# Decoder layer with routed experts on one core: order of the work between the last cross attention and the experts

## The chip, the cores and the metric

One Trainium2 chip, one of its cores. The metric is the device time of one execution in microseconds (us), lower is better; the median of several runs is given. The engines are TensorE (PE in the profile, with PEld for its weight loads), VectorE (DVE), ScalarE (ACT), GpSimd (POOL) and SyncE (SP), which only starts transfers. Each has its own queue and runs it in order; they meet by semaphores.

## The reference

All in float32, for 16 sequences of 256 tokens and 256 features:

```python
x = x + L0_attn(layernorm(x))        # causal linear attention with exp features, 4 heads of 64,
                                     # then y -> relu(norm(y) @ W1 + b1) @ W2 + b2
x = x + L0_xattn(layernorm(x), ctx)  # q from x, k and v from ctx; softmax(q k^T / 16) v + bv
x = x + L0_ffn(layernorm(x))         # 16 experts, the best 2 of each token
# L0_ffn:
probs = softmax(xf @ Wg.T); topw, topi = top_k(probs, 2); topw = topw / topw.sum(-1)
out = sum over e of gates[:, e] * ((silu(xf @ W1[e]) * (xf @ W3[e])) @ W2[e])
```

## The kernel before, in words

A tile is 128 tokens; a sequence has TS = 2 of them, there are NSEQ = 16 sequences, numbered 0 to 15, and X holds the whole stream in SBUF. The kernel has three parts.

**Turns.** Turn i works on four sequences at once (`in_turns`, L360 and on): attention of sequence i (a), feed forward of i-1 (f), cross attention of i-2 (b), choice and places of i-3 (r). Each engine has a function `turn` with its own order of these pieces, written out by hand. Most products are made in three: a float32 value is split into hi and rest in a format for faster products (`mm3`), hi by ScalarE, rest by VectorE (`rest`). Turn 16 (`last_ffn`) has no attention; it makes the feed forward of 15, the cross attention of 14 and the places of 13. There TensorE would pause, so `keep_clock(bank, n)` (L809) issues n products of a mask with the identity, whose result nobody reads; each gives two records in the trace.

In a turn GpSimd adds the value bias bv of the cross attention to X (`add_bias`, L640), splits the next context (`split_ctx`), ranks the chosen experts (`place_rows`), and takes roots of variances for the layer norms (`root`, L633; norm 3 is the one ahead of the router). It also scatters each token's normalised row, with its number and gate, to its place in a list in DRAM that is ordered by expert (`store_rows`, L699): four indirect DMAs per sequence, two tiles by two choices, each waiting for places, gates and rows.

**Close.** `close()` on each engine has what is left: the cross attention of sequence 15, and router, choice, places and rows of 14 and 15. It works by halves (tiles), without splitting. TensorE: value product of the context, one filler, X of sequence 14 turned for its router (bank 4), the halves of xn2 turned, router of 14, queries, scores, the counts of the choice of 14 (`count_choices`), then pr turned, the weighted values, X of 15 turned, its router, three fillers, its counts. VectorE: the row constants of the scores (`row_constants`, L1722, one fused product and sum for each tile), logits and choice of 14 (`logits_in`, `choose`, `one_hot`, `row_shifts`), the scores' row maxima to snmax, gates and places of 14 (`gates`, `place_own`), then X with its statistics for 15 (L1936 to L1943), and the same choice and places for 15. ScalarE copies out of PSUM, takes the exps (`score_exp`, `gap_exp`) and writes the rows to be scattered (`whole_rows`). GpSimd's `close` (L764):

```python
store_rows(NSEQ - 3, range(1))
add_bias(NSEQ - 1, bv_sb, xn2_ready, xbv_ready, NSEQ + 1)
root(3, NSEQ - 2, eps_ln)
store_rows(NSEQ - 3, range(1, TS))
for r in (NSEQ - 2, NSEQ - 1):
    keep_rows(r)
store_rows(NSEQ - 2, range(1))
pool.wait_ge(egap_ready, NSEQ - 1)
pool.wait_ge(rows_kept, NSEQ - 2 + TS)
root(3, NSEQ - 1, eps_ln)
store_rows(NSEQ - 2, range(1, TS))
store_rows(NSEQ - 1)
```

**Plan and experts.** VectorE works out from the counts which expert each tile of 128 places belongs to (row_g, L1975; expert_i, L1984); TensorE issues nine fillers ahead of this plan's two small products and ten after it (L1240). When all scatters have landed SyncE loads the first tiles of rows, and then TensorE goes through 79 tiles: rows turned (L1197), up products, hidden turned (L1219), down products. GpSimd adds each result into the output by a scatter.

What sets the order: the hand written order of each queue, the semaphores, and PSUM banks (the router of 14 writes bank 5, the counts too).

Of the kernel before, what the change touches and what calls it, by code (L numbers as in the profile page):

```python
# [37 lines left out]
ALU = mybir.AluOpType  # L38
# [3 lines left out]
P = 128  # L42
# [5 lines left out]
def decoder(nc, x, ctxT, WqT, WkT, Wv, Wo, omegaT, W1, b1, W2, b2, gamma, beta,  # L48
# [52 lines left out]
    with ExitStack() as stack:  # L101
# [497 lines left out]
        def _(pool):  # L599
# [40 lines left out]
            def add_bias(seq, row, after, done, count=None):  # L640

                hold(pool, after, seq + 1 if count is None else count)
                xs = X[:, tiles_of(seq), :]
                pool.tensor_tensor(xs, xs, row[:, :].unsqueeze(1).broadcast_to([P, TS, D]), ALU.add).then_inc(done, 1)
# [68 lines left out]
            def turn(i, a, f, b, r, nxt):  # L713
# [28 lines left out]
                last_ffn = isinstance(i, int) and i == NSEQ  # L742
                if b is not None:
                    add_bias(b, bv_sb, xn2_ready, xbv_ready)
                    hold(pool, v2_ps, b + 1)
                    pool.wait_ge(score_ps, b + 1)
                    if last_ffn:
                        pool.wait_ge(fT_ready, NSEQ * 4)
                    split_ctx(b + 1)
# [14 lines left out]
            def close():  # L764

                store_rows(NSEQ - 3, range(1))
                add_bias(NSEQ - 1, bv_sb, xn2_ready, xbv_ready, NSEQ + 1)
                root(3, NSEQ - 2, eps_ln)
                store_rows(NSEQ - 3, range(1, TS))
                for r in (NSEQ - 2, NSEQ - 1):  # L770
# [7 lines that stand above are left out]
# [27 lines left out]
        def _(pe):  # L805
# [124 lines left out]
            def turn(i, a, f, b, r, nxt):  # L930
# [33 lines left out]
                if b is not None:  # L964
# [5 lines left out]
                    if last_ffn:  # L970
                        keep_clock(0, 8)
# [4 lines left out]
                if last_ffn:  # L976
                    keep_clock(0, 2)
# [132 lines left out]
            def close():  # L1110
# [4 lines left out]
                pe.wait_ge(x2_ready, NSEQ - 1)  # L1115
                turn_tiles(4, X[:, rows_of:rows_of + TS, :]).then_inc(xn3T_ps, 1)
# [3 lines left out]
                pe.wait_ge(counts_ready, NSEQ - 2)  # L1120
                pe.wait_ge(xn3T_ready, NSEQ - 1)
                for t in range(TS):
                    last = router_half(t, ps[:, 5, S + t * NE:S + (t + 1) * NE])
                last.then_inc(logit_ps, 1)
                for t in range(TS):
# [6 lines left out]
                    last.then_inc(q_ps, 1)  # L1132
                for t in range(TS):
# [5 lines left out]
                count_choices(NSEQ - 2)  # L1139
# [4 lines left out]
                for t in range(TS):  # L1144
# [4 lines left out]
                    last.then_inc(av_ps, 1)  # L1149
                for t in range(TS):  # L1150
                    pe.wait_ge(x2_ready, NSEQ + t)
                    turn_half(t, X[:, rows_of + TS + t, :]).then_inc(xn3T_ps, 1)
                for t in range(TS):
# [86 lines left out]
            keep_clock(2, 10)  # L1240
# [27 lines left out]
        def _(act):  # L1268
# [205 lines left out]
            def close():  # L1474
                copy_router_rows(NSEQ - 2, 4)
# [10 lines left out]
                gap_exp(NSEQ - 2)  # L1486
                act.wait_ge(zT_ps, NSEQ)
                whole_rows(rows_cross, NSEQ - 2, 0)
# [4 lines left out]
                whole_rows(rows_cross, NSEQ - 2, 1)  # L1493
# [76 lines left out]
        def _(dve):  # L1570
# [332 lines left out]
            def close():  # L1903
# [12 lines left out]
                logits_in(r, 5, S)  # L1916
                hold(dve, logit_ready, r + 1)
                choose(r)
                one_hot(r)
                row_shifts(r)  # L1920
# [6 lines left out]
                dve.wait_ge(egap_ready, r + 1)  # L1927
                gates(r)
                place_own(r)
# [14 lines left out]
                last.then_inc(mv_ready[3], 1)  # L1944
                logits_in(b, 2)
# [162 lines left out]
```

## Time and profile before

| | us |
|---|---|
| median of 3 runs | 811.09 |
| lowest, highest | 810.24, 813.86 |
| the profiled execution | 813.92 |
| its span | 812.1 |
| busy: PE, DVE, ACT, POOL | 792.2, 593.3, 435.6, 394.8 |
| mean granted clock of TensorE | 0.992 of full |

The profile is of one execution, and its rows give times from the start of the span. TensorE is busy 98% of the span, but its pauses, and the time at a lower granted clock, lie close together, around the close and the start of the experts (600 to 642 us). A row of the timeline gives start, duration, engine, line, what is written from what, how many instructions were merged, and in brackets how long the engine stood idle before it and who released it. Matmul records overlap, since they are pipelined; their distance is what they cost.

### The profile page before, as it was taken

The page shows a single profiled execution, that of the slowest core. Times are in us where ns is not written, and L with a number is a line of the kernel's source. Part 1 is how long each engine was busy: PE and PEld are TensorE (multiplying, and loading weights), DVE is VectorE, ACT ScalarE, POOL GpSimd, SP SyncE. Part 2 cuts the span into 40 slices and gives each one's busy share as a digit, 9 for nine tenths or more (in the row PEclk, how much of TensorE's full clock was granted, in tenths as well). Part 3 has the DMA queues.
Part 4 walks back from the last instruction along what each step waited for, and adds up shares of the span by engine and source line. Part 5 has one row for each costly group of instructions (what it writes and reads, how often), then busy time and mean ns, then how long its engine had stood idle before and what let it go on. Part 6 is the DMA issues. An engine that isn't in the chain of part 4 may idle for free.

```text
span 812.1 us, 20962 instructions
## 1 busy us (share of the span) xinstructions
PE 792.2 (98%) x5907; PEld 752.9 (93%) x5908; DVE 593.3 (73%) x1719; ACT 435.6 (54%) x1193; POOL 394.8 (49%) x561
## 2 busy tenths in 40 slices
PE   9999999999999999999999999999998899999995
PEld 8899999999999999999999999999896799999994
DVE  4757777888787877888887877888667466666663
ACT  4473554637274454637274554637145377667673
POOL 2432134444434354443534344443436258787876
PEclk9999999999999999999999999999999999999998
DMA  9787673755748283755748283757869357787880
GB/s 269 255 285 236 207 259 113 255 192 192 250 139 293 92 307 112 254 189 178 264 141 289 95 307 108 258 199 287 322 261 334 111 103 134 121 131 127 132 137 2
DMA packets 105961, 161.19 MB, mean 198 GB/s; under 512 B 10704, under 2 KB 69648, under 8 KB 105040
## 3 DMA queue, kind: packets, MB, share of 16 engines
q1 hardware_dynamic: 80544, 132.89, 47.8%
q0 software_dynamic: 14800, 17.61, 11.9%
q10 hardware_dynamic: 10576, 10.19, 4.7%
q8 instruction: 20, 0.33, 0.2%
q14 instruction: 21, 0.17, 0.1%
HBM read 50.14 MB, written 112.47 MB: 200 GB/s over the span
## 4 chain that ended last, share of the span: by engine, by line
PE 87%; DVE 5%; ACT 3%; issue 2%; POOL 1%; DMA 1%; POOLq 0%; DVEq 0%; SPq 0%; ACTq 0%
PE ps L807 75%; PE ps L818 5%; PE ps L1041 3%; PE ps L1197 2%; PE ps L1219 2%; ACT phi L1335 1%; ACT fT_hi L1348 1%; ACT relu_v L1349 1%; DVE pr L1724 1%; DVE xn_attn L1590 0%; DMA expert_rows<-relu_v,place_i 0%; DVE stat L1579 0%; DVE snmax L1791 0%; DVE fT_lo L1597 0%; POOL expert_rows L710 0%
## 5 line engine op out<-in xcount | busy, mean ns | idle before, releaser
L798 POOL DMA_INDIRECT out<-narrow,sidx x79 | 122.8, 1554 | 47.4 <-DVE sidx L2037 22.4
L1270 ACT ACTIVATE xn3T<-ps 128x512 f32<-128x512 f32 (+1 forms) x18 | 10.3, 574 | 141.4 <-PE ps L818 136.1
L807 PE MATMUL ps<-w_hi,fT_hi 128*128 128x256 f32 x256 | 79.9, 312 | 0.3
L1335 ACT ACTIVATE phi<-ps,nmax 128x128 f32<-128x128 f32 x256 | 73.5, 381 | 8.1 <-DVE nmax L1741 7.6
L1597 DVE TENSOR_TENSOR fT_lo<-relu_v,fT_hi 128x512 fp32r<-128x512 f32 x64 | 51.4, 802 | 31.9 <-ACT relu_v L1349 31.7
L807 PE MATMUL ps<-w_hi,fT_lo 128*128 128x256 f32 x256 | 72.4, 283 | 0.0
L807 PE MATMUL ps<-w_lo,fT_hi 128*128 128x256 f32 x256 | 72.2, 282 | 0.0
L1349 ACT ACTIVATE relu_v<-ps,b_sb 128x256 f32<-128x256 f32 x128 | 69.0, 539 | 0.0
L1348 ACT ACTIVATE fT_hi<-ps,b_sb 128x256 fp32r<-128x256 f32 x128 | 68.0, 531 | 1.0 <-PE ps L807 1.0
L807 PE MATMUL ps<-hT_hi,w_hi 128*128 128x256 f32 x256 | 67.2, 284 | 0.0
L807 PE MATMUL ps<-hT_hi,w_lo 128*128 128x256 f32 x256 | 67.0, 283 | 0.0
L636 POOL TENSOR_TENSOR veps<-mv,eps_ln 128x2 f32<-128x2 f32 x48 | 10.9, 228 | 109.4 <-DVE mv L1583 108.1
L710 POOL DMA_INDIRECT expert_rows<-rows,place_i x56 | 55.6, 992 | 15.3 <-issue 15.3
L807 PE MATMUL ps<-e_hi,xgT_hi 128*128 x158 | 58.5, 371 | 0.7 <-issue 0.6
L2031 DVE TENSOR_TENSOR hidT_lo<-ps,hidT_hi 128x256 fp32r<-128x256 f32 x79 | 33.6, 425 | 32.5 <-ACT hidT_hi L1270 31.3
L2019 DVE TENSOR_TENSOR xgT_lo<-ps,xgT_hi 128x256 fp32r<-128x256 f32 x79 | 33.5, 424 | 25.3 <-ACT xgT_hi L1270 24.4
L807 PE MATMUL ps<-hT_lo,w_hi 128*128 128x256 f32 x256 | 51.6, 284 | 0.0
L807 PE MATMUL ps<-e_lo,xgT_hi 128*128 x158 | 51.6, 328 | 0.0
L649 POOL CAST ctx_hi<-ctx_raw 128x512 fp32r<-128x512 f32 x16 | 10.4, 651 | 82.7 <-DMA ctx_raw<-in_ctxT 64.7
L807 PEld LDWEIGHTS ps<-w_hi,fT_hi 128*128 128x128 f32 x256 | 48.6, 190 | 1.9 <-DVE fT_lo L1597 1.4
L1270 ACT ACTIVATE xgT_hi<-ps 128x256 fp32r<-128x256 f32 x79 | 30.3, 384 | 36.5 <-issue 26.5
L807 PEld LDWEIGHTS ps<-hT_hi,w_hi 128*128 128x128 f32 x256 | 49.2, 192 | 0.0
(329 smaller groups left out, 2761.0 us busy)
## 6 DMA issues: line engine op xcount, KB each, us to landing
expert_rows<-zero_rows SPq DMA_DIRECT2D x16, 4352.0 KB, 16.2
narrow<-expert_rows ACTq DMA_DIRECT2D x71, 136.0 KB
expert_up_hi<-X SPq DMA_DIRECT2D x16, 352.0 KB, 2.7
e_hi<-expert_up_hi SPq DMA_DIRECT2D x2, 2816.0 KB, 10.0
part_raw<-in_E SPq DMA_DIRECT2D x30, 176.0 KB
expert_up_lo<-part_raw SPq DMA_DIRECT2D x15, 352.0 KB, 3.1
e_lo<-expert_up_lo SPq DMA_DIRECT2D x2, 2464.0 KB, 13.0
X<-in_x SPq DMA_DIRECT2D x16, 256.0 KB, 3.4
```

The lines of the kernel that those rows point to most:

```text
L710: pool.indirect_dma_start(row_dram, bass.IndirectOffsetOnAxis(place_i[:, buffer_of(r), j, t:t + 1], 0), kept[:, t, j, :], None).then_inc(p ...
L798: pool.indirect_dma_start(out_rows, bass.IndirectOffsetOnAxis(sidx[:, u:u + 1], 0), yg[:, u, :], None, bounds_check=NT * P - 1, oob_is_err ...
L807: return pe.matmul(out_, lhsT, rhs, start=start, stop=stop)
L818: last = pe.transpose(ps[:, bank, lo:lo + P], src[:, t, c * P:(c + 1) * P], ident[:, :])
L1041: last = pe.transpose(ps[:, g0 + h // 2, h % 2 * S + t * P:h % 2 * S + (t + 1) * P], phi[:, g0 + t, h, :], ident[:, :])
L1270: return act.activation(out_, in_, ACT.Copy)
L1335: last = act.activation(phi[:, g, h, :], ps[:, g, h * M:(h + 1) * M], ACT.Exp, bias=nmax[:, g, h:h + 1])
L1348: act.activation(fT[0][:, 2 * g + n, :], bank(bank_no)[:, n, :], ACT.Relu, bias=bias)
L1349: last = act.activation(relu[:, g % 2, n, :], bank(bank_no)[:, n, :], ACT.Relu, bias=bias)
L1597: dve.tensor_tensor(dst, whole, hi.bitcast(F32), ALU.subtract).then_inc(done, 1)
L2019: dve.tensor_tensor(xgT[1][:, u % 2], ps[:, u % 2, 0:D].rearrange("p (c s) -> p c s", c=DC), xgT[0][:, u % 2].bitcast(F32), ALU.subtract). ...
L2031: dve.tensor_tensor(hidT[1][:, u % 2], ps[:, 4 + u % 2, 0:2 * P].rearrange("p (c s) -> p c s", c=2), hidT[0][:, u % 2].bitcast(F32), ALU.s ...
```

## The change

It moves and edits pieces of turn 16 and of `close`:

- GpSimd: in turn 16 it waits for the rest of hT of sequence 15 (`hT_ready`) before adding the value bias to sequence 14. In `close` it no longer adds the bias of sequence 15.
- VectorE: the three operations from maximum to snmax of the scores come before logits and choice of 14; then VectorE adds the value bias of 15 itself; gates and places of 14 come after the statistics of X of 15.
- TensorE: fillers of turn 16 are 4 and 1 instead of 8 and 2; in `close` X of 14 is turned after the queries, its router comes after the scores and its counts after the weighted values; a filler stands between the two halves of X of 15; the fillers after the plan's products are 13 instead of 10.
- ScalarE: the copy of xn3T of 14 comes after the queries' copies; `gap_exp` and both `whole_rows` of 14 come after the copies of prT.

```diff
 # GpSimd, turn and close
                 last_ffn = isinstance(i, int) and i == NSEQ
+                if last_ffn:
+                    pool.wait_ge(hT_ready, NSEQ)
                 if b is not None:
                     add_bias(b, bv_sb, xn2_ready, xbv_ready)
...
                 store_rows(NSEQ - 3, range(1))
-                add_bias(NSEQ - 1, bv_sb, xn2_ready, xbv_ready, NSEQ + 1)
                 root(3, NSEQ - 2, eps_ln)
 # TensorE, turn, close and ahead of the experts
                     if last_ffn:
-                        keep_clock(0, 8)
+                        keep_clock(0, 4)
                     pe.wait_ge(xn2_ready, b + 1)
...
                 if last_ffn:
-                    keep_clock(0, 2)
+                    keep_clock(0, 1)
...
                 keep_clock(3, 1)
-                pe.wait_ge(x2_ready, NSEQ - 1)
-                turn_tiles(4, X[:, rows_of:rows_of + TS, :]).then_inc(xn3T_ps, 1)
                 for t in range(TS):
                     pe.wait_ge(xn2_ready, NSEQ + t)
                     turn_half(t, xn2[:, t, :]).then_inc(xn2T_ps, 1)
-                pe.wait_ge(counts_ready, NSEQ - 2)
-                pe.wait_ge(xn3T_ready, NSEQ - 1)
-                for t in range(TS):
-                    last = router_half(t, ps[:, 5, S + t * NE:S + (t + 1) * NE])
-                last.then_inc(logit_ps, 1)
...
                     last.then_inc(q_ps, 1)
+                pe.wait_ge(x2_ready, NSEQ - 1)
+                turn_tiles(4, X[:, rows_of:rows_of + TS, :]).then_inc(xn3T_ps, 1)
...
                     last.then_inc(score_ps, 1)
-                count_choices(NSEQ - 2)
+                pe.wait_ge(counts_ready, NSEQ - 2)
+                pe.wait_ge(xn3T_ready, NSEQ - 1)
+                for t in range(TS):
+                    last = router_half(t, ps[:, 5, S + t * NE:S + (t + 1) * NE])
+                last.then_inc(logit_ps, 1)
...
                     last.then_inc(av_ps, 1)
+                count_choices(NSEQ - 2)
                 for t in range(TS):
                     pe.wait_ge(x2_ready, NSEQ + t)
                     turn_half(t, X[:, rows_of + TS + t, :]).then_inc(xn3T_ps, 1)
+                    keep_clock(4, 1 - t)
...
-            keep_clock(2, 10)
+            keep_clock(2, 13)
 # ScalarE, close
-                copy_router_rows(NSEQ - 2, 4)
...
                     last.then_inc(qT_hi, 1)
+                copy_router_rows(NSEQ - 2, 4)
+                for t in range(TS):
+                    score_exp(t)
+                for t in range(TS):
+                    turned_half(t, prT_ps, 2 + t, last_prT, prT_hi)
                 gap_exp(NSEQ - 2)
                 act.wait_ge(zT_ps, NSEQ)
-                whole_rows(rows_cross, NSEQ - 2, 0)
-                for t in range(TS):
-                    score_exp(t)
-                for t in range(TS):
-                    turned_half(t, prT_ps, 2 + t, last_prT, prT_hi)
-                whole_rows(rows_cross, NSEQ - 2, 1)
+                for t in range(TS):
+                    whole_rows(rows_cross, NSEQ - 2, t)
 # VectorE, close
                 then_shifted(dve.tensor_tensor(row_bias[:, :], xrow[:, :], brow_sb[:, :], ALU.add))
+                for t in range(TS):
+                    one = slice(t, t + 1)
+                    dve.wait_ge(score_ps, NSEQ + t)
+                    then_shifted(dve.tensor_reduce(smax[:, one], ps[:, t, 0:S], AX_X, ALU.max, negate=True))
+                    then_shifted(dve.tensor_tensor(row_max_of[:, one], smax[:, one], row_bias[:, one], ALU.subtract))
+                    dve.tensor_tensor(snmax[:, one], row_max_of[:, one], row_bias[:, one], ALU.add).then_inc(snmax_ready, 1)
+                dve.tensor_tensor(X[:, tiles_of(b), :], X[:, tiles_of(b), :],
+                                  bv_sb[:, :].unsqueeze(1).broadcast_to([P, TS, D]), ALU.add).then_inc(xbv_ready, 1)
                 logits_in(r, 5, S)
...
                 row_shifts(r)
-                for t in range(TS):
...
-                dve.wait_ge(egap_ready, r + 1)
-                gates(r)
-                place_own(r)
                 dve.wait_ge(pr_ready, NSEQ + 1)
...
                 last.then_inc(mv_ready[3], 1)
+                dve.wait_ge(egap_ready, r + 1)
+                gates(r)
+                place_own(r)
                 logits_in(b, 2)
```

## Rows read from the trace of the kernel before

**Rows 1.** The page: the chain that ended last, shares of the span by engine

```profile
PE 87%; DVE 5%; ACT 3%; issue 2%; POOL 1%; DMA 1%; POOLq 0%; DVEq 0%; SPq 0%; ACTq 0%
```

**Rows 2.** The chain of waits: start us, us, engine, tile, line, count

```profile
587.91 11.78 PE ps L807 x96
...
630.86 3.22 DMA expert_rows<-relu_v,place_i
```

**Rows 3.** TensorE in order of time: start us, us, line, out<-in, count [idle before<-releaser]

```profile
582.38 3.69 PE L807 MATMUL ps<-mask,ident 128*128 128x256 f32 x16 [0.46 <-DVE logits L1719]
...
586.34 1.03 PE L807 MATMUL ps<-mask,ident 128*128 128x256 f32 x4
```

**Rows 4.** VectorE in order of time, last layer norms before the tail

```profile
584.05 0.71 DVE L1590 TENSOR_SCALAR xn<-X,mv,rstd 128x256 f32<-128x256 f32 x2
585.42 1.59 DVE L1590 TENSOR_SCALAR y<-y,mv,rstd 128x256 f32<-128x256 f32 x2 [0.66 <-POOL rstd L638]
```

**Rows 5.** GpSimd in order of time, the bias of the second last sequence

```profile
585.27 1.26 POOL L644 TENSOR_TENSOR X<-X,bv_sb 128x512 f32<-128x512 f32 x1
```

**Rows 6.** VectorE in order of time, the tail

```profile
610.08 1.97 DVE L1724 SCALAR_TENSOR_TENSOR pr<-xn,wrow 128x256 f32<-128x256 f32 x1
...
612.42 0.19 DVE L1719 COPY logits<-ps 128x32 f32<-128x32 f32 x1 [0.18 <-DVE row_bias L1915]
...
614.39 0.42 DVE L1924 TENSOR_REDUCE smax<-ps 128x1 f32<-128x256 f32 x1
...
615.91 0.16 DVE L1688 TENSOR_SCALAR gden<-egap 128x2 f32<-128x2 f32 x1
...
617.34 0.17 DVE L1714 CAST place_i<-place_f 128x4 int32<-128x4 f32 x1
...
620.35 0.48 DVE L1936 SCALAR_TENSOR_TENSOR X<-ps,rsum,X 128x256 f32<-128x256 f32 x1 [0.55 <-PE ps L807]
...
622.57 0.19 DVE L1719 COPY logits<-ps 128x32 f32<-128x32 f32 x1 [0.77 <-PE ps L807]
...
625.98 0.17 DVE L1714 CAST place_i<-place_f 128x4 int32<-128x4 f32 x1
```

**Rows 7.** TensorE in order of time, the tail and the fillers

```profile
609.37 1.04 PE L807 MATMUL ps<-wg_sb,xn3T 128*128 128x16 f32 x8
610.25 2.03 PE L807 MATMUL ps<-raw_w,xwq_whole 128*128 128x128 f32 x16
612.12 2.01 PE L807 MATMUL ps<-ctx_raw,raw_w 128*128 128x256 f32 x8
...
615.92 0.44 PE L927 MATMUL ps<-ident,pr 128*128 128x128 f32 x2 [1.25 <-ACT pr L1467]
...
622.27 1.54 PE L807 MATMUL ps<-mask,ident 128*128 128x256 f32 x6
...
624.67 4.13 PE L807 MATMUL ps<-mask,ident 128*128 128x256 f32 x18
629.48 0.38 PE L807 MATMUL ps<-ident,expert_of_tile 128*1 128x128 f32 x2 [0.68 <-DVE row_g L1975]
...
630.78 4.55 PE L807 MATMUL ps<-mask,ident 128*128 128x256 f32 x20 [0.71 <-DVE expert_i L1984]
636.39 0.44 PE L1197 MATMUL ps<-ident,narrow 128*128 128x128 f32 x2 [1.05 <-DMA narrow<-expert_rows]
```

**Rows 8.** GpSimd in order of time, the tail

```profile
618.42 0.98 POOL L710 DMA_INDIRECT expert_rows<-xn_attn,place_i  x1 [2.71 <-ACT xn_attn L1462]
...
622.25 0.72 POOL L638 TENSOR_TENSOR rstd<-veps,halfneg 128x2 f32<-128x2 f32 x1
...
627.06 0.96 POOL L710 DMA_INDIRECT expert_rows<-relu_v,place_i  x1 [1.28 <-ACT relu_v L1462]
```

**Rows 9.** Two stretches: us, busy of PE, PEld, DVE, ACT, POOL, granted clock, DMA

```profile
617.50:620.50 3.00, 3.00 (x9) 2.15 (x7) 1.30 (x6) 0.71 (x2) 1.77 (x2) 0.50 1.01 325
638.00:641.00 3.00, 3.00 (x13) 2.93 (x12) 1.18 (x4) 0.70 (x2) 0.00 (x0) 0.50 0.61 175
```

More of the change, by code:

```diff
@@ L638, in root, with add_bias @@
                 pool.tensor_tensor(rstd[:, n, :], veps[:, n, :], halfneg[:, :], ALU.pow).then_inc(rstd_ready[n], 1)
-            def add_bias(seq, row, after, done, count=None):
-                hold(pool, after, seq + 1 if count is None else count)
+            def add_bias(seq, row, after, done):
+                hold(pool, after, seq + 1)
                 xs = X[:, tiles_of(seq), :]
@@ L1485, in close @@
                     last.then_inc(qT_hi, 1)
-                gap_exp(NSEQ - 2)
-                act.wait_ge(zT_ps, NSEQ)
-                whole_rows(rows_cross, NSEQ - 2, 0)
+                copy_router_rows(NSEQ - 2, 4)
                 for t in range(TS):
@@ L1492, in close @@
                     turned_half(t, prT_ps, 2 + t, last_prT, prT_hi)
-                whole_rows(rows_cross, NSEQ - 2, 1)
+                gap_exp(NSEQ - 2)
+                act.wait_ge(zT_ps, NSEQ)
+                for t in range(TS):
+                    whole_rows(rows_cross, NSEQ - 2, t)
                 act.wait_ge(logit_ps, NSEQ - 1)
@@ L1915, in close @@
                 then_shifted(dve.tensor_tensor(row_bias[:, :], xrow[:, :], brow_sb[:, :], ALU.add))
[L1916 to L1920, printed above, removed]
                 for t in range(TS):
@@ L1926, in close @@
                     dve.tensor_tensor(snmax[:, one], row_max_of[:, one], row_bias[:, one], ALU.add).then_inc(snmax_ready, 1)
-                dve.wait_ge(egap_ready, r + 1)
-                gates(r)
-                place_own(r)
+                dve.tensor_tensor(X[:, tiles_of(b), :], X[:, tiles_of(b), :],
+                                  bv_sb[:, :].unsqueeze(1).broadcast_to([P, TS, D]), ALU.add).then_inc(xbv_ready, 1)
+                logits_in(r, 5, S)
+                hold(dve, logit_ready, r + 1)
+                choose(r)
+                one_hot(r)
+                row_shifts(r)
                 dve.wait_ge(pr_ready, NSEQ + 1)
```

## The prediction

> **What bounds the kernel now.** I read the page's chain first: TensorE holds 87% of it [rows 1]. Only time on that chain counts, and the change touches two stretches of it, 582 to 588 us and 606 to 638 us, and the fillers between router and experts. So I then read the chain and each engine's timeline there. From 587.91 TensorE streams without a gap for 11.78 us (and, with its transposes, until the tail begins near 607.6) [rows 2]: what starts that run earlier moves everything behind it. In the tail the chain hops between VectorE, TensorE and ScalarE, and it ends through GpSimd: four scatters of the last sequence from 627.06, the last landing 3.22 us after 630.86 [rows 2, 8]. Nothing of the experts can start before that landing, and a scatter can start only when GpSimd's queue and VectorE's places both allow. This queue is the thing to follow.
>
> TensorE's granted clock is at its lower level (0.50, that is 1.2 of 2.4 GHz) in 617.5 to 620.5 and in 638 to 641, busy throughout [rows 9]. Before the first it had idled 1.25 us up to 615.92, before the second 1.05 us up to 636.39; the idle times of 0.68 and 0.71 us before 629.48 and 630.78 were followed by no fall in the pieces shown, since the ten fillers from 630.78 run at 0.455 us each as do the nine before (4.13 us) [rows 7].
>
> **Step 1, the last feed forward: 8 to 4 and 2 to 1 fillers, GpSimd's bias held.** The eight fillers take 3.69 us from 582.38 to 586.07 [rows 3]. What they wait out, xn2, is ready at 584.05 + 0.71 = 584.76 [rows 4]. Four end near 582.38 + 1.98 = 584.4, so the transposes can start at about 584.8 instead of 585.90 (rows overlap): 1.1 us earlier. VectorE's y takes 1.59 us though its twin xn takes 0.71; GpSimd's bias runs from 585.27 for 1.26 beside it [rows 4, 5]. Held until hT's rest is written, about 588, the bias falls into a stretch where VectorE waits, and y ends at 585.42 + 0.71 = 586.13. Then xn2's rest (0.7, the same 512 elements per partition) ends near 586.8, and TensorE goes on there instead of 587.91. The two fillers of 1.03 us at 586.34 [rows 3] become one inside the wait. Gain 1.1 us: at least 0.6, if only the fillers' part comes, at most 1.2. Behind the new wait on GpSimd's queue stand only the bias and the next context split, which waits for the last relu rests anyway; the bias is read only in the tail. TensorE gets pauses of about 0.5 and 0.4 us, shorter than the 0.71 that cost nothing [rows 7].
>
> **Step 2, the cross attention ahead.** All times from here are in the old count; step 1 shifts them together. The router (1.04 us at 609.37) no longer stands before the queries (610.25) [rows 7]. xn2's halves are turned at 608.5 to 609.3; ScalarE, no longer held by xn3T's copy, finishes the first at 609.4, so the queries start 0.8 us earlier, at 609.45, and end near 611.4. X's four transposes (0.45) now stand before the scores, so the first score is complete near 612.9 and the second near 613.8; before it was 614.1 (612.12 + 2.01) [rows 7]. Here the gain is only 0.3.
>
> The gain is on VectorE. The second row constant took 1.97 us from 610.08 [rows 6]; without a GpSimd bias beside it I price it like the neighbouring halves, 0.4, and VectorE is idle at 610.8, waiting for scores. Its old choice (logits 612.42 to maximum 614.39, 1.97 us) [rows 6] no longer precedes the maxima. They start at 612.9 and 613.8 instead of 614.39 and 0.8 later, each 0.8 us long, so the last is out at 614.65 instead of 616.0: 1.35 us earlier. Exp, transposes and the two products follow, and TensorE's pause before the second transposes shrinks from 1.25 us [rows 7] to about 0.6, so the products should stay at full clock. They would be complete near 616.8 and 617.7.
>
> But VectorE now has the bias, for which the nearest row is 0.71 (512 elements per partition, SBUF to SBUF) [rows 4], with 1.26 (GpSimd's own time) [rows 5] as the upper bound and 0.35 (half of 0.71) as the lower; I take 0.7. Bias and choice fill it from 614.6 to 615.3 and to 617.3. X's halves therefore start at 617.55 and 618.6 (1.05 apart, the cadence of addition and statistics); the second started at 620.35 before [rows 6]. That is 1.75 us early, and bn_aggr would end at 620.05.
>
> **Step 3, what is behind it.** Gates and places of the second last sequence took from 615.91 to 617.51, 1.6 us [rows 6]; now they start at 620.05 and end at 621.65. The last logits could be read from 621.1, but VectorE takes them at 621.75: 0.8 us before 622.57 [rows 6], against a gain of 1.75 at X.
>
> GpSimd's order is unchanged: two scatters of sequence 14, then the last root, then two more scatters of 14, then four of 15. The first pair ran at 618.42, 0.9 us after its places [rows 6, 8]. Now it starts at 621.65 + 0.9 = 622.55; with 1.3 us from scatter to scatter it ends at 624.8, and only then comes the last root (0.2 + 0.72), out at 625.8. Before, it was out at 622.25 + 0.72 = 622.97 [rows 8]. So rstd is 2.8 us late. The slack in front of it is small: ScalarE's exp of the gap needs it, then gates and places follow. The last place_i went from rstd 622.97 to 625.98; now exp (0.5), gates and places (1.6) make it 625.8 + 2.0 = 627.8, 1.8 late. GpSimd itself is free at the same time: 625.8 + 0.5 + 2.3 + 0.3 = 628.9, against 627.06 [rows 6, 8]. Both ways give +1.8. The least I give it is 0 (if places come at the earliest, before the second X half), the most 2.6 (if VectorE's queue slips by another 0.8).
>
> By the Trainium skill (SBUF — State Buffer, section "SBUF: two separate sides") VectorE can hold the port pair that GpSimd needs to write descriptors; taken strictly, some seven small VectorE operations of 0.17 us beside the four scatters would add up to 1.2 us more, and the sum would be 812.8. Against this stands that in this trace the scatter at 618.42 took 0.98 us with VectorE nearly idle and the one at 627.06 took 0.96 beside VectorE's plan arithmetic [rows 8].
>
> **Step 4, fillers.** In the tail two fillers of the close stay, one is added between X's halves; it ends before the second half arrives and costs nothing (0.45 if that cover goes). The three after the router would now end at about 622.0 while the choice that they cover is ready at 623.7: a pause of 1.7 us, where the six records of 1.54 us at 622.27 left 0.79 before [rows 7]. After it come nine fillers of 4.13 us, and then a pause before row_g, which moves to 629.48 + 1.8 = 631.3: at least 1.8 us. Both are longer than the 1.05 and 1.25 us that went before a fall. So I expect the lower clock in the first half of the last fillers. Thirteen take 13 × 0.455 = 5.9 us at full clock from 630.78 + 1.8 = 632.6, to 638.5; the rows come at 636.39 + 1.8 = 638.2 [rows 7]: just covered. With some 3 us of it at half clock [rows 9] they end at 640.1, 1.9 after the first rows. As the second tile's rows arrive about 0.5 later than the first anyway, the experts lose 1.4. In exchange they begin at full clock, and the 3 us at 0.50 in 638 to 641 [rows 9], worth 1.5 to 1.7, are saved: 1.6.
>
> **Sum.** -1.1 (step 1) + 1.8 (step 3, with the gains of step 2 already in it) + 1.4 (fillers overrun) - 1.6 (clock) = +0.5 us. The profiled execution took 813.92 us; it would take 814.4. The median of the runs is 2.8 us lower, at 811.09, and a constant offset I carry over: **811.6 us**. Of this kernel's time a measurement can tell about 0.5%, 4.1 us, from nothing.
>
> **Rivals.** *Covered fillers*: the clock stays up in the fillers, for instance because two filler groups lie near the pauses. Then the overrun is nil: -1.1 + 1.8 - 1.6 = -0.9, 810.2 us. For it speaks that pauses of 0.7 us did nothing; against it, that these are more than twice as long.
>
> *The gain reaches the end*: places of 14 come early enough that GpSimd's root isn't late (0 instead of 1.8), with the clock up: -1.1 - 1.6 + 0 = -2.7, and 0.5 of that is lost to fillers that now outlast the rows: 808.9. Against it stands the order on VectorE's queue, in which gates come behind bn_aggr.
>
> *Slower*: the same queue lateness, and the fall of the clock comes so late that it lasts into the experts: the overrun is paid and the 1.6 isn't regained, -1.1 + 1.8 + 1.4 = +2.1, 813.2 us. It decides at the granted clock of the first expert product: below 1 there, this case holds. To be slower by over 4 us it would need the whole 2.6 of step 3 and a failed step 1 as well (+2.6 + 1.4 = +4.0).
>
> *Step 1 does nothing*: TensorE's run starts at 587.9 as before, because something unseen releases it. Then 812.7. Against: both named releasers are in the rows.
>
> **Chances.** Forecast 0.38, covered fillers 0.27, gain to the end 0.12, slower 0.15, step 1 empty 0.08. All lie within 4.1 us of 811.09, so same is 0.89; 0.06 faster for a gain further on that I don't see, 0.05 slower for the extreme above. Range 808.8 to 814.0: the outer cases with the runs' own spread.
>
> **What would show it.** Right: TensorE's long run starting 1.1 us earlier; y at 0.71; the second row constant at 0.4; the second X half about 2.8 us earlier in absolute time; the last rstd about 1.7 later; first scatter of the last sequence about 0.7 later; granted clock 0.5 in the last fillers and 1.0 at the first expert product. Wrong: the last root before the first pair of scatters, or X's second half still near 619 or later, which would mean that the clock fell there too.

## The result and the profile after

The kernel after takes 815.59 us in the median of 15 runs (814.05 to 818.12), the kernel before, 15 runs beside it, 812.62 (810.24 to 816.0). The ratio is 1.0038, 95% interval 1.0025 to 1.0051: 3 us slower, above the forecast 811.6 and above the top of its range, 814.0. The difference is under the 4.1 us that the prediction takes as the least to be told from nothing, so its "same" came true, but the interval is clear of zero. A second comparison on another chip gave 817.17 against 813.85, ratio 1.0033 (1.0014 to 1.0051). In what follows a difference of runs in us is the ratio's, times 812.

The profiled execution took 816.94 us. The page's span line and the line of TensorE:

```profile
span 815.2 us, 20957 instructions
...
PE 790.9 (97%) x5905; PEld 751.2 (92%) x5906; DVE 591.0 (73%) x1720; ACT 435.3 (53%) x1193; POOL 392.5 (48%) x560
```

Both traces have to be counted from the same event, since what came before turn 16 differs by 2.2 us between these two executions; in the other executions of both kernels it is as scattered, and in no order that follows the kernel. I take the copy of turn 16's logits, 582.04 us in the trace of before and 584.20 in that of after, and write such times as "+x". TensorE of after, in order of time, around step 1:

```profile
584.53 1.97 PE L808 MATMUL ps<-mask,ident 128*128 128x256 f32 x8 [0.47 <-DVE logits L1721]
...
587.47 0.60 PE L808 MATMUL ps<-mask,ident 128*128 128x256 f32 x2
...
589.04 0.39 PE L808 MATMUL ps<-xn2T_hi,xwq_hi 128*128 128x256 f32 x1
```

Its long run now starts at 589.04, +4.84, against 587.91, +5.87, before [rows 2]: 1.03 us earlier. VectorE, whose y is no longer held by GpSimd's bias (0.73 us instead of 1.59 [rows 4]):

```profile
584.20 0.19 DVE L1721 COPY logits<-ps 128x32 f32<-128x32 f32 x1
...
587.58 0.73 DVE L1592 TENSOR_SCALAR y<-y,mv,rstd 128x256 f32<-128x256 f32 x2 [0.66 <-POOL rstd L638]
```

VectorE in the tail:

```profile
611.20 0.42 DVE L1726 SCALAR_TENSOR_TENSOR pr<-xn,wrow 128x256 f32<-128x256 f32 x1
...
614.81 0.42 DVE L1921 TENSOR_REDUCE smax<-ps 128x1 f32<-128x256 f32 x1
...
615.56 0.68 DVE L1924 TENSOR_TENSOR X<-X,bv_sb 128x512 f32<-128x512 f32 x1
...
619.36 0.47 DVE L1937 SCALAR_TENSOR_TENSOR X<-ps,rsum,X 128x256 f32<-128x256 f32 x1
...
622.11 0.17 DVE L1716 CAST place_i<-place_f 128x4 int32<-128x4 f32 x1
...
622.53 0.19 DVE L1721 COPY logits<-ps 128x32 f32<-128x32 f32 x1 [0.17 <-DVE carry L1717]
...
626.50 0.16 DVE L1673 SCALAR_TENSOR_TENSOR row_shift<-mv,rstd 128x2 f32<-128x2 f32 x1 [1.99 <-POOL rstd L638]
...
628.50 0.17 DVE L1716 CAST place_i<-place_f 128x4 int32<-128x4 f32 x1
```

The second row constant takes 0.42 us where it took 1.97 [rows 6] (the line shown is the second of the two). The second maximum comes at +30.6, the bias takes 0.68, X's second half starts at +35.2 (before: +38.3), but the places of sequence 14 come at +37.9 (before: 617.34, +35.3) and the last logits at +38.3 (before: +40.5). Then VectorE idles 1.99 us for the last root. GpSimd shows why:

```profile
623.20 0.97 POOL L710 DMA_INDIRECT expert_rows<-xn_attn,place_i  x1 [7.77 <-DVE place_i L1716]
624.47 0.97 POOL L710 DMA_INDIRECT expert_rows<-xn_attn,place_i  x1 [0.30 <-issue]
...
625.75 0.72 POOL L638 TENSOR_TENSOR rstd<-veps,halfneg 128x2 f32<-128x2 f32 x1
626.97 1.04 POOL L710 DMA_INDIRECT expert_rows<-xn_attn,place_i  x1 [0.51 <-issue]
...
629.58 0.96 POOL L710 DMA_INDIRECT expert_rows<-relu_v,place_i  x1 [0.31 <-issue]
```

It idled 7.77 us for the places of 14, issued their first pair, and only then took the last root: rstd starts at +41.6, against 622.25, +40.2, before [rows 8]. The first scatter of the last sequence is at +45.4, before +45.0. So the whole gain ahead of this point is gone, and 0.4 us with it. TensorE from the scores to the first expert product:

```profile
612.88 1.89 PE L808 MATMUL ps<-ctx_raw,raw_w 128*128 128x256 f32 x8
...
616.66 1.96 PE L808 MATMUL ps<-raw_xq,raw_xv 128*128 128x256 f32 x8
...
621.26 1.54 PE L808 MATMUL ps<-mask,ident 128*128 128x256 f32 x6
...
624.57 0.19 PE L808 MATMUL ps<-oh,before 128*128 128x32 bf16 x1 [1.76 <-DVE oh L1678]
...
624.63 4.13 PE L808 MATMUL ps<-mask,ident 128*128 128x256 f32 x18
632.00 0.59 PE L808 MATMUL ps<-ident,expert_of_tile 128*1 128x128 f32 x2 [3.24 <-DVE row_g L1979]
...
633.72 8.03 PE L808 MATMUL ps<-mask,ident 128*128 128x256 f32 x26 [0.71 <-DVE expert_i L1988]
641.59 0.60 PE L1199 MATMUL ps<-ident,narrow 128*128 128x128 f32 x4
642.59 0.42 PE L808 MATMUL ps<-e_hi,xgT_hi 128*128 x1 [0.41 <-ACT xgT_hi L1272]
```

The weighted values take 1.96 us, at full clock (before: 3.30 us, most of it at the lower clock). Then come a pause of 1.76 us, nine fillers, a pause of 3.24 us, and thirteen fillers in 8.03 us, 0.62 us each instead of 0.455 [rows 7]. The rows are turned right behind them, with no wait for the rows. The first expert product is at 642.59, +58.4, against +55.6 before. The stretches with their granted clock (us; busy PE, PEld, DVE, ACT, POOL; clock; DMA share; GB/s):

```profile
616.00:622.00 6.00, 5.32 (x30) 4.16 (x31) 4.70 (x27) 3.48 (x10) 0.00 (x0) 1.00 1.00 337
630.00:632.00 2.00, 0.00 (x1) 0.01 (x2) 1.72 (x13) 0.00 (x0) 1.50 (x2) 0.83 0.30 109
632.00:638.00 6.00, 5.29 (x14) 3.84 (x15) 1.37 (x10) 0.00 (x0) 2.73 (x4) 0.50 0.20 72
...
642.00:644.00 2.00, 1.59 (x11) 1.40 (x10) 0.76 (x2) 0.81 (x3) 0.00 (x0) 1.00 0.51 141
```

In stretches of 0.1 us the lower clock holds from 631.3 to 638.1, that is 6.8 us: it fell 0.7 us before the pause of 3.24 us ended. The experts start at 1.00.

### The profile page after: what moved, and what is told of

Read it like the earlier page. It is cut to its first block and busy times, and to the rows that moved or that the text cites. A ratio compares the mean times of both kernels' runs of the same rounds, so it can differ in the third digit from the quotient of the medians.

```text
span 815.2 us, 20957 instructions
## 1 busy us (share of the span) xinstructions
PE 790.9 (97%) x5905; PEld 751.2 (92%) x5906; DVE 591.0 (73%) x1720; ACT 435.3 (53%) x1193; POOL 392.5 (48%) x560
## 5 line engine op out<-in xcount | busy, mean ns | idle before, releaser
L710 POOL DMA_INDIRECT expert_rows<-rows,place_i x56 | 55.6, 993 | 15.2 <-issue 15.2
L1272 ACT ACTIVATE xgT_hi<-ps 128x256 fp32r<-128x256 f32 x79 | 30.2, 384 | 39.2 <-issue 26.5
L808 PEld LDWEIGHTS ps<-hT_hi,w_hi 128*128 128x128 f32 x256 | 49.2, 192 | 0.0
L808 PEld LDWEIGHTS ps<-hT_hi,w_lo 128*128 128x128 f32 x256 | 49.1, 192 | 0.0
```

What stands on the lines that cost most here:

```text
L710: pool.indirect_dma_start(row_dram, bass.IndirectOffsetOnAxis(place_i[:, buffer_of(r), j, t:t + 1], 0), kept[:, t, j, :], None).then_inc(p ...
L808: return pe.matmul(out_, lhsT, rhs, start=start, stop=stop)
L1272: return act.activation(out_, in_, ACT.Copy)
```

## The experiments

Ten kernels were run (before and after among them), several more than once. In the table "third tile" is the start of the first product of the third expert tile, in us from turn 16's logits copy; the fall of the clock is one between turn 16 and that tile. In every trace the clock is lower as well for 8 to 12 us at the very end, and in a_pauses, a_root and a_root_2 for 3.4 us near 32 us, ahead of the stretch counted here. From the third tile to the end all traces have 168.8 to 170.9 us, in no order that follows the edits.

| kernel | third tile | fall of the clock, trace by trace | runs against before (95%) |
|---|---|---|---|
| before, 4 traces | 60.44, 58.88, 59.14, 58.27 | at pr in all four; at the experts in the first | 1 |
| after, after_2 | 61.66, 60.48 | at the last fillers, for 6.8 and 3.4 us | 1.0038, 1.0033 |
| a_fill10, a_fill10_2 | 59.47, 60.60 | at the last fillers, for 3.4 and 6.8 us | 1.0046 (1.0030 to 1.0062), 1.0024 (1.0009 to 1.0039) |
| a_order | 61.43 | at the last fillers, for 6.8 us | 1.0038 (1.0022 to 1.0054) |
| a_pauses | 59.10 | none | 1.0023 (1.0009 to 1.0036) |
| a_gates | 57.96 | from the last router on | 1.0020 (1.0005 to 1.0035) |
| a_root, a_root_2 | 57.29, 57.25 | none | 0.9998 (0.9984 to 1.0011), 0.9995 (0.9982 to 1.0008) |
| b_step1, b_step1_2 | 55.95, 58.49 | none; at pr | 0.9991 (0.9976 to 1.0007), 0.9980 (0.9966 to 0.9994) |
| b_bias | 57.69 | at the experts | 0.9975 (0.9956 to 0.9994) |
| b_cover | 56.11 | none | 0.9975 (0.9958 to 0.9992) |

**a_fill10 and a_fill10_2: the fillers ahead of the experts back to ten.**

```diff
-            keep_clock(2, 13)
+            keep_clock(2, 10)
```

after_2 is the kernel after with no edit.

> The kernel after with 10 fillers ahead of the experts instead of 13, as before. Theory A (the fillers outlast the rows because they run at the lower clock): the last three run at full clock in the trace of after, 0.43 us each, so the first expert product comes 1.3 us earlier against the plan, and the run is 1.3 us faster than after (about +1.7 us to before). Theory B (what is lost lies ahead of turn 16, or in the row path): the first product does not move by more than 0.3 us against expert_i, and the time is that of after (+3.0).

> The kernel after, unchanged, beside a_fill10_2 on one chip. Theory A: from turn 16's logits copy expert_i again at 49.2 us, the first expert product at 58.4 and the third tile's at 61.7; granted clock at its lower level from about 2.9 us after the pause of 3.2 us begins until more than 3 us after its end. Theory J (that trace was an exception): the 13 fillers take 5.9 us and the first product comes at 56.2.

> a_fill10 again, since its first trace put the third tile 2.2 us before that of after while the runs showed no gain. Theory A: the runs too are 1.3 us below those of after_2. Theory K (the clock falls again later or the expert part gives it back): no difference in the runs, and the stretch from the third tile to the end is longer by the same 1.3 us or more.

The ten fillers took 6.24 and 6.93 us, the thirteen of after_2 7.26; the first product came at +56.2 and +57.3, against +58.4 and +57.2. The edit is worth 1.0 us in the mean of two traces each, but two traces of one kernel differ by as much, by how long the clock stayed low: 3.4 us in one trace of each kernel and 6.8 in the other. Like is to be compared with like: the third tile is 1.0 us earlier between the two short ones and 1.1 between the two long ones. The runs say 0.8 us on the one chip (816.33 against 817.17, intervals that overlap); on the other a_fill10, in five runs, is no better than after (1.0046). The direction is as theory A has it in the traces, its 1.3 us isn't shown, and the runs do not tell it from nothing.

**a_pauses: the pauses filled.**

```diff
-                keep_clock(3, 3)
+                keep_clock(3, 7)
...
-            keep_clock(2, 9)
+            keep_clock(2, 16)
```

> The kernel after with the two pauses filled: 7 instead of 3 fillers after the last router and 16 instead of 9 after the last counts. Theory A (the pauses of 1.76 and 3.24 us lower the clock, and that makes the 13 fillers last 8.0 us): granted clock 1.0 until the experts, the 13 fillers take 5.9 us, the first expert product comes 2.0 us earlier, time 2.0 us below after. Theory D (the clock falls for another reason, or the rows are late themselves): less than 0.5 us.

TensorE, in order of time:

```profile
631.51 0.38 PE L808 MATMUL ps<-ident,expert_of_tile 128*1 128x128 f32 x2 [0.22 <-DVE row_g L1979]
...
632.81 5.85 PE L808 MATMUL ps<-mask,ident 128*128 128x256 f32 x26 [0.71 <-DVE expert_i L1988]
638.50 0.60 PE L1199 MATMUL ps<-ident,narrow 128*128 128x128 f32 x4
639.51 0.42 PE L808 MATMUL ps<-e_hi,xgT_hi 128*128 x1 [0.41 <-ACT xgT_hi L1272]
```

Thirteen fillers in 5.85 us and no fall from turn 16 to the experts, the third tile 2.0 us ahead of the mean of after. In the runs the ratio is 1.0023, slower than before by 1.9 us, so about 1 us of the loss seems gone (the intervals of the two ratios overlap), and not the 2.0 of theory A. With the pauses filled the clock did not fall, where it fell in all five traces that have them, and the overrun was real. With it gone, something else still costs.

**a_root and a_root_2: the last root ahead of the first pair of scatters.**

```diff
-                store_rows(NSEQ - 2, range(1))
                 pool.wait_ge(egap_ready, NSEQ - 1)
                 pool.wait_ge(rows_kept, NSEQ - 2 + TS)
                 root(3, NSEQ - 1, eps_ln)
+                store_rows(NSEQ - 2, range(1))
```

> The kernel after with GpSimd's last root ahead of the first two scatters of sequence 14. Theory A (the root was late because it stood behind two scatters): rstd comes 4.5 us earlier (about 1.1 us after bn_aggr), expert_i 2 to 2.5 us earlier, the first scatter of the last sequence 1.3 us earlier (four scatters and no root before it); the pause of 3.2 us before the plan's products shrinks under 1.2, the fillers run at full clock, and the first expert product comes 2 to 2.5 us earlier: about 813.3, that is +0.7 to before. Theory B (places, not the root, set it): rows move by less than 0.4 us, time 815.

> a_root again. Theory A: third tile at 57.3 us after the logits copy, no fall of the clock, runs 2.5 to 3.5 us below those of after and within 1 us of before; above b_step1_2 by 0.5 to 1.5 us, since the scatters of 15 start 1.3 us later there (44.2 against 42.9).

GpSimd of a_root in order of time, and TensorE after it (584.83 is its logits copy):

```profile
621.64 0.19 POOL L636 TENSOR_TENSOR veps<-mv,eps_ln 128x2 f32<-128x2 f32 x1 [5.54 <-DVE mv L1944]
621.91 0.72 POOL L638 TENSOR_TENSOR rstd<-veps,halfneg 128x2 f32<-128x2 f32 x1
623.87 1.05 POOL L710 DMA_INDIRECT expert_rows<-xn_attn,place_i  x1 [1.24 <-DVE place_i L1716]
...
627.76 0.96 POOL L710 DMA_INDIRECT expert_rows<-xn_attn,place_i  x1 [0.30 <-issue]
```

```profile
630.18 0.38 PE L808 MATMUL ps<-ident,expert_of_tile 128*1 128x128 f32 x2 [0.75 <-DVE row_g L1979]
...
631.48 5.85 PE L808 MATMUL ps<-mask,ident 128*128 128x256 f32 x26 [0.71 <-DVE expert_i L1988]
```

rstd starts at +37.1 instead of +41.6, expert_i comes at +46.3 instead of +49.2 and +48.7, the first scatter of 15 at +44.2 instead of +45.4. The pause before the plan's products is 0.75 us instead of 3.24, no fall follows (the pause of 1.76 us after the router stays, and alone brings none in either trace), and 13 fillers take 5.85 us. The third tile is 3.8 us earlier than in after, and the runs are level with before. One swap of two calls takes back the whole loss, on two chips. It is the late root that costs, by itself and by the pause it makes on TensorE. Against the traces of before, though, a_root's third tile is 1.9 us early, and its runs are only level: see what is left open.

**a_gates: gates and places of 14 back ahead of X.**

```diff
+                dve.wait_ge(egap_ready, r + 1)
+                gates(r)
+                place_own(r)
                 dve.wait_ge(pr_ready, NSEQ + 1)
...
                 last.then_inc(mv_ready[3], 1)
-                dve.wait_ge(egap_ready, r + 1)
-                gates(r)
-                place_own(r)
```

> The kernel after with gates and places of sequence 14 back ahead of X on VectorE (TensorE's order unchanged). Theory A (the late places hold GpSimd's first pair, and with it the last root): places at 35.5 us after turn 16's logits copy instead of 37.9, first scatter of 14 at 36.4 instead of 39.0, X's second half later, at 36.7, the last root's rstd at about 39.0 instead of 41.5, first scatter of 15 at 43.4 instead of 45.4, third tile at about 57.2; in the runs 3 us below after, no slower than before by more than 0.5 us. Theory B (the lateness in the runs has a cause outside of this stretch): still 2 us or more above before.

GpSimd in order of time (582.20 is the logits copy):

```profile
618.80 0.97 POOL L710 DMA_INDIRECT expert_rows<-xn_attn,place_i  x1 [5.38 <-DVE place_i L1716]
...
621.07 0.21 POOL L636 TENSOR_TENSOR veps<-mv,eps_ln 128x2 f32<-128x2 f32 x1
621.36 0.72 POOL L638 TENSOR_TENSOR rstd<-veps,halfneg 128x2 f32<-128x2 f32 x1
622.58 1.04 POOL L710 DMA_INDIRECT expert_rows<-xn_attn,place_i  x1 [0.51 <-issue]
623.92 0.96 POOL L710 DMA_INDIRECT expert_rows<-xn_attn,place_i  x1 [0.30 <-issue]
```

Places at +35.5, the first scatter at +36.6, rstd at +39.2: as theory A has it. X's second half is at +37.0. TensorE now pauses 2.13 us for X, the clock falls 2.2 us after that pause, from the last router on, and the first scatter of 15 comes at +44.2, 0.8 later than worked out. Third tile +58.0. The runs gain 1.4 us on after, not 3, and stay 1.6 above before.

**a_order: the new order of the close alone, with 8 and 2 fillers, no wait in turn 16, ten fillers.**

```diff
-                if last_ffn:
-                    pool.wait_ge(hT_ready, NSEQ)
...
-                        keep_clock(0, 4)
+                        keep_clock(0, 8)
...
-                    keep_clock(0, 1)
+                    keep_clock(0, 2)
...
-            keep_clock(2, 13)
+            keep_clock(2, 10)
```

> The order of the close and the bias alone: the kernel after with 8 and 2 fillers and without the wait in turn 16, and with 10 fillers ahead of the experts. Theory A: 1.05 us more than a_fill10, because step 1 is undone, everything else counted from y's end as there; about +4 us to before. Theory I (step 1 is worth nothing once rows are late): the time of a_fill10.

Everything from xn2 on is 1.0 us later than in a_fill10 (X's second half at +36.2, rstd at +42.6), the third tile at +61.4. Of the two traces of a_fill10 the one that also had the clock low for 6.8 us is the one to set beside it: 60.6, 0.8 us earlier. In the runs 816.24 against 813.21: slower by 3.1, where theory A said 4 and the two comparisons of a_fill10 gave 3.7 and 1.9, so the runs do not decide between A and I. The order of the close and the bias make the kernel slower, with the fillers of turn 16 and those ahead of the experts as they were (the one between X's halves stays).

**b_step1 and b_step1_2: step 1 alone, on the kernel before.**

```diff
+                if last_ffn:
+                    pool.wait_ge(hT_ready, NSEQ)
...
-                        keep_clock(0, 8)
+                        keep_clock(0, 4)
...
-                    keep_clock(0, 2)
+                    keep_clock(0, 1)
```

> The kernel before with step 1 alone: 4 and 1 fillers in turn 16 and GpSimd's bias held until hT_ready. Theory A: TensorE's long run starts 1.05 us earlier counted from the logits copy, and the time is 1.0 us below before. Theory C (shifts of this kind are eaten by something later, or any such edit costs about 2 us ahead of turn 16): the same as before or slower.

> b_step1 again, beside a_gates and a_root_2 on one chip. Its first trace had neither fall of the clock and a third tile at 55.95 us, but the runs gained only 0.7. Theory M (whether the clock falls at the products of pr differs from run to run, in before too): in the mean 1 us below before, and a trace with or without the fall (third tile 55.9 to 58.5). Theory C (the gain is eaten later): no difference to before, with the stretch from the third tile to the end above 170.5 us.

The long run starts 1.03 us earlier after the logits copy, in both traces. The runs gain 0.7 and 1.6 us (the second clear of zero), 1.2 in the mean. The two traces differ by 2.5 us in the third tile, for two reasons. In the first the clock did not fall at the products of pr, behind the same pause of 1.24 us as before, in the second it did: X's second half is 1.44 us later there, and so is the first scatter of 15. The other 1.1 us is the landing of the last scatter, in the chain of waits of b_step1 and of b_step1_2:

```profile
628.51 2.44 DMA expert_rows<-relu_v,place_i
```

```profile
630.85 3.56 DMA expert_rows<-relu_v,place_i
```

No edit here was aimed at it. In the four traces of before it is 3.22, 3.06, 3.21 and 2.43 us, in both of a_root 2.4, in b_bias and b_cover 3.4 and 3.5. The prediction took the 3.22 us of its one trace as given.

**before_2 to before_4: the kernel before, with no edit.**

> The kernel before, unchanged, for a second trace. Theory E (the first trace of before holds two falls of the clock that its other executions often don't have): the products of pr at full clock (X's second half 1.1 us earlier after the logits copy of turn 16 than the 38.31 us of the first trace) and the third tile's first product at about 57 us after that copy, instead of 60.44. Theory F (the first trace is typical): again 38.3 and 60.4.

> The kernel before once more, as before_2: a third trace, to see which of the two falls of the clock comes back.

> The kernel before once more: a fourth trace. Theory E: the fall of the clock at the products of pr as in three traces (X's second half at 38.3 to 38.7 us after the logits copy), and again none ahead of the experts or one, by chance; third tile at 59.0 or 60.4.

The stretches of before_2 with their granted clock:

```profile
619.00:622.00 3.00, 3.00 (x9) 2.25 (x8) 1.17 (x6) 0.71 (x2) 1.77 (x2) 0.50 1.01 336
632.00:638.00 6.00, 4.62 (x21) 3.79 (x22) 0.85 (x6) 0.00 (x0) 2.96 (x5) 1.00 0.32 99
638.00:641.00 3.00, 2.67 (x16) 2.18 (x17) 1.07 (x3) 1.37 (x4) 0.69 (x1) 1.00 0.72 203
```

The fall at the products of pr is in all four traces of before. The one at the first expert tiles is in the first alone. First products of the first and of the third tile, in before and in before_2:

```profile
637.64 0.42 PE L807 MATMUL ps<-e_hi,xgT_hi 128*128 x1 [0.22 <-issue]
...
642.48 0.41 PE L807 MATMUL ps<-e_hi,xgT_hi 128*128 x1
```

```profile
639.14 0.42 PE L807 MATMUL ps<-e_hi,xgT_hi 128*128 x1 [0.22 <-issue]
...
642.41 0.41 PE L807 MATMUL ps<-e_hi,xgT_hi 128*128 x1
```

Where it is, the third tile starts 4.84 us after the first; where it isn't, 3.27: it costs 1.57 us.

**b_bias and b_cover: step 1 and the bias on VectorE, the old order kept, then 12 fillers instead of 10.**

```diff
-                add_bias(NSEQ - 1, bv_sb, xn2_ready, xbv_ready, NSEQ + 1)
...
                     dve.tensor_tensor(snmax[:, one], row_max_of[:, one], row_bias[:, one], ALU.add).then_inc(snmax_ready, 1)
+                dve.tensor_tensor(X[:, tiles_of(b), :], X[:, tiles_of(b), :],
+                                  bv_sb[:, :].unsqueeze(1).broadcast_to([P, TS, D]), ALU.add).then_inc(xbv_ready, 1)
                 dve.wait_ge(egap_ready, r + 1)
```

The edit is shown against b_step1; b_cover has `keep_clock(2, 12)` besides.

> b_step1 with the value bias of the last sequence on VectorE after snmax, the order of the close unchanged. Theory G (the bias beside VectorE's row constants costs the chain): the second row constant takes 0.4 us, the router's logits are read 1.4 us earlier, snmax comes 0.3 to 0.5 us earlier (TensorE's scores then gate it) and so do the last places; time 0.3 to 0.5 us below b_step1. Theory H (VectorE's added 0.7 us is on the path, since gates and places of 14 follow it): no gain or 0.3 us of loss.

> b_bias with 12 fillers ahead of the experts instead of 10. Theory A: the 12 end about 51.3 us after the logits copy, before the rows at 51.6, no fall follows, and the first two tiles run at full clock: 1.5 us below b_bias where that had the fall, 0.7 in the mean; about 810.8 if before is 813.2. Theory L (the fall comes from elsewhere): the same as b_bias.

VectorE of b_bias in order of time (582.97 is its logits copy):

```profile
609.67 0.39 DVE L1725 SCALAR_TENSOR_TENSOR pr<-xn,wrow 128x256 f32<-128x256 f32 x1
...
609.99 0.42 DVE L1725 SCALAR_TENSOR_TENSOR pr<-xn,wrow 128x256 f32<-128x256 f32 x1
...
610.79 0.19 DVE L1720 COPY logits<-ps 128x32 f32<-128x32 f32 x1 [0.17 <-DVE row_bias L1916]
```

The logits of 14 are read at +27.8, 1.5 us ahead of b_step1, the maximum 1.1 ahead, the places of 14 at +33.9 and of 15 at +41.0: 0.8 ahead of b_step1's faster trace. TensorE's pause before the transposes of pr is 0.57 us instead of 1.24, and the clock stays up there in both kernels. In b_bias it fell at the experts, behind a pause of 1.22 us; with two more fillers this pause is 0.52 and there is no fall: third tile +56.1. But both kernels have the same ratio, 0.9975, so the two fillers are not shown to be worth anything in the runs. Both kernels are 2.0 us below before by the ratio, where after is 3 above. That the bias on VectorE adds to step 1 is shown in the traces; in the runs the intervals overlap those of b_step1 and b_step1_2.

## Why the prediction was wrong

Of the signs that it named, all came: the long run earlier, y at 0.73, the row constant at 0.42, X's second half 3.1 us earlier, the last root 1.3 us later (1.7 forecast), the first scatter of 15 0.4 us later (0.7 forecast), the clock at 0.50 in the last fillers and at 1.00 at the first expert product. The path was right; the sum put on it was not.

**Step 1** held: 1.1 us forecast, 1.03 in the traces, with the mechanism named (y at 0.73).

**Step 2** held to 0.4 us. Counted as in the text, from before and shifted by step 1: second maximum forecast at 613.8, measured 612.65 + 1.03 = 613.7; bias 0.7, measured 0.68; X's second half 618.6, measured 618.2; the products at full clock.

**Step 3** held in kind and was a little too large. The places of 14 (forecast to end at 621.65, measured 621.2) held GpSimd's pair, the pair held the root, the root held VectorE for 1.99 us. a_root shows that this is the cause. In the old count the first scatter of 15 came 1.2 us later than in the mean of four traces of before (45.38 + 1.03 against 45.19), 1.4 later than in the one that the sum was made from, not 1.8. Scatters beside VectorE's choice took 0.96 to 1.04 us, as before: the 1.2 us that the rule of the Trainium skill (SBUF — State Buffer, "SBUF: two separate sides") would have added, taken strictly, did not come.

**Step 4** is the step that failed, in two of its terms. The first is the -1.6 us that I let the experts regain: it was hardly there to regain. I took a fall of the clock that one execution showed for a property of the kernel; three more traces don't have it. In the mean of four it is worth 0.4 us. The second is the overrun, 2.1 us and not 1.4: from the first scatter of 15 to the first product the four traces of before need 9.9 to 10.6 us and both of a_root 9.8, after needed 13.0 and 11.8. The clock was low for 6.8 us in one trace of after and 3.4 in the other, and I had priced 3, the length of the stretches read in rows 9; the falls themselves lasted 3.4 us there.

To the first product my sum was -1.1 + 1.8 + 1.4 = +2.1, and +2.3 was measured (57.8 against 55.5). That they meet is in part luck: the scatter was 0.5 us less late than forecast and the overrun 0.7 us larger. The last term brought the sum to +0.5; the third tile, where that term should have shown, came 1.9 us late (61.1 against 59.2). This is the rival called slower, in its size; its test, a clock below 1 at the first product, was wrong, because it tied the missing gain to a fall in after instead of to no fall in before.

The base was off too. Of the 4.0 us between forecast and median, 1.5 are there before any edit: before had 811.09 us in the three runs that the forecast stands on, and 812.62 in fifteen. The rest is +3.0 for +0.5. Of these 2.5 us the regain is 1.2 and the overrun 0.7, step 3 takes 0.5 back, and 1.1 is what the runs have above the traces.

**Left open.** The runs lose 3.1 and 2.7 us, the traces of the stretch 1.9. The first trace of b_step1, a_root, a_gates, a_pauses and a_fill10 too come out 1.5 to 3.4 us worse against before in the runs than their third tiles say; b_bias and b_step1_2 do not. The likeliest place is before itself: an execution without the fall at pr would have its third tile near 57, and four traces needn't have met it. The mean granted clock that every run has on record fits this. In the 110 runs of before on four chips it is 0.9936 in the mean, and 0.9923 in the 27 of after: 0.0013 less (0.0014 on the chip of after_2 alone). A mean that is lower by 0.001 is 1.6 us of 812 more at the lower level, so after has 2.1 to 2.3 us more. The traces of the stretch have only 0.9 us more (5.1 in the mean of after's two, 4.3 in that of before's four). a_root has 2.1 us less than before in its runs where its traces have 4.3 less, and a_gates 3.6 more where its trace has 0.9 less. So, set against the other kernels, the executions of before spend less time at the lower clock than its four traces say. Counted at half a us of work for each us at the lower clock (the falls of 3.4 us cost 1.44 and 1.57), this makes up 0.5 us in a_pauses, 1.0 to 1.8 in a_root, b_step1, after_2 and a_fill10, 2.2 in a_gates, and nothing in b_bias and b_step1_2. That is an estimate from those clocks, which also hold the 8 to 12 us at the end of the kernel; what remains is not explained.

## What to carry to other kernels

When work is moved between engines in order, look for the queue that receives its results: here GpSimd had two scatters and a root in a fixed order, and a gain of 3 us on VectorE turned into an idle GpSimd and then a late root. Something short that others wait for now (a root of 1 us) belongs ahead of something longer that is needed only later (here two scatters). And a stall seen in one trace isn't a gain in the bank: take a second trace of the kernel before, before counting it.

## What was not expected of the hardware

A pause of TensorE does not settle by its length alone whether the granted clock falls. Behind 1.25 us ahead of pr it fell in four traces of before and one of b_step1, and not in another of b_step1; behind 1.76 us after the router it did not fall in either trace of a_root; behind 0.95 to 1.49 us ahead of the experts it fell in one trace of before and in b_bias, and not in before_2, before_3 and b_step1_2; at 3.24 us it fell in all five traces that have such a pause, and behind the 2.13 us of a_gates in its one trace. Nor does the pause settle how long the clock stays low. Ten of the thirteen falls between turn 16 and the experts lasted 3.4 us. The other three lasted 6.8 us, all at the pause of 3.24 us (after, a_fill10_2, a_order), and in these three the clock fell 0.3 to 0.7 us before the pause ended; in after_2 and a_fill10 it fell 0.7 and 1.7 us after the end.

The landing of the last scatter took 2.4 to 3.6 us from trace to trace, of one and the same kernel too (b_step1 2.44, b_step1_2 3.56).

Two operations of VectorE from SBUF to SBUF, the second row constant (1.97 us) and y (1.59 us), went to 0.42 and 0.73 us when GpSimd's addition of 1.27 us beside them was moved; moved to VectorE, the same addition took 0.68 us. The prediction had counted on both.
